# A two-layer scan and mixture-of-experts kernel: expert biases through a selection matmul, C's product on GpSimd, and a second variance worked out from the first

## The reference

```python
x = L0_attn_x
xn = _layernorm(x)                                   # (x - m) / sqrt(v + 1e-5)
x = x + scan_layer(xn) + experts_0(xn)               # layer 0
xn = _layernorm(x)
x = x + heads(xn) + experts_1(xn)                    # layer 1

# scan_layer: 16 states n per channel
h_n[t] = exp(delta[t] * A_n) * h_n[t-1] + delta[t] * x[t] * B_n[t]
y[t]   = sum_n C_n[t] * h_n[t]
return y + D_param * x

# experts_l: 8 experts, the best 2 per token
h   = gelu(x @ w1[n] + b1[n])                        # 128 -> 512
out = h @ w2[n] + b2[n]                              # 512 -> 128
# experts_1 alone normalises its input once more:
xn2 = (x - mu) / sqrt(var + 1e-5) * gamma + beta
```

## Time and profile before

| | us |
|---|---|
| median of 3 runs | 1023.39 (1023.01 to 1023.41) |
| the profiled execution, its time | 1015.58 |
| its span in the trace | 1013.8 |
| busy: PE, DVE | 699.5 (69%), 777.8 (77%) |
| busy: ACT, POOL | 526.4 (52%), 445.8 (44%) |
| mean granted TensorE clock | 0.809 of full speed |

### The profile page before, as it was taken

The page is one execution under the profiler, slowest core; times in us unless marked ns, Lnnn a source line. Parts: engine busy times, 40 slices in busy tenths (PEclk is TensorE's granted clock), DMA queues, the critical chain, the costliest instruction groups (busy, mean ns, idle before and its releaser), DMA issues.

```text
span 1013.8 us, 18728 instructions
## 1 busy us (share of the span) xinstructions
PE 699.5 (69%) x5012; PEld 470.6 (46%) x5012; DVE 777.8 (77%) x1700; ACT 526.4 (52%) x1131; POOL 445.8 (44%) x444
## 2 busy tenths in 40 slices
PE   1975176789998999889901451259789789788760
PEld 0422022256565555556601351237667567567550
DVE  4898999989889888989657729535786775876857
ACT  2678423387768776875304520054664564655620
POOL 1356385634454444444202551525555555554330
PEclk9865578899999999999965555568798797797775
DMA  8332132434444444343150020001111011111108
GB/s 243 110 95 68 40 92 76 128 107 127 117 130 112 121 117 122 112 124 109 61 158 21 1 83 1 11 21 30 31 31 33 29 29 30 31 35 28 23 10 248
DMA packets 68658, 78.56 MB, mean 77 GB/s; under 512 B 10354, under 2 KB 43576, under 8 KB 68564
## 3 DMA queue, kind: packets, MB, share of 16 engines
q1 hardware_dynamic: 55124, 57.42, 19.7%
q0 software_dynamic: 9216, 17.85, 7.0%
q10 hardware_dynamic: 4224, 2.10, 0.7%
HBM read 62.39 MB, written 15.99 MB: 77 GB/s over the span
## 4 chain that ended last, share of the span: by engine, by line
PE 40%; DVE 34%; issue 12%; ACT 6%; POOL 3%; DMA 2%; SPq 1%; another core or an unknown queue 1%; DVEq 0%; ACTq 0%; POOLq 0%
PE pb L767 7%; PE po L812 6%; PE pb L912 6%; DVE work L1196 5%; DVE x L1084 3%; PE ph L793 3%; PE po L810 3%; DVE work L1205 2%; DVE work L1343 2%; PE ph L795 2%; PE ph L794 2%; DVE pb L1188 2%; PE po L817 2%; PE pb L903 2%; PE po L819 1%
## 5 line engine op out<-in xcount | busy, mean ns | idle before, releaser
L465 POOL DMA_INDIRECT results<-res,pair_of x144 | 156.0, 1084 | 305.8 <-DVE res L1159 283.2
L593 ACT ACTIVATE arena<-ph,b 128x128 f32<-128x128 f32 x576 | 164.7, 372 | 142.6 <-PE ph L795 87.4
L459 POOL DMA_INDIRECT xrow<-rows,row_of x144 | 159.5, 1108 | 64.2 <-issue 42.1
L1196 DVE TENSOR_TENSOR_SCAN work<-decay,pb 128x512 f32<-128x512 f32 x128 | 154.7, 1208 | 0.1
L767 PE MATMUL pb<-work,idf 128*128 128x512 f32 x256 | 140.7, 638 | 5.2 <-DVE work L1205 4.4
L793 PE MATMUL ph<-xrT,w1h 128*128 128x128 f16 x576 | 123.7, 233 | 25.4 <-issue 15.0
L794 PE MATMUL ph<-xrT,w1h 128*128 128x128 f16 x576 | 122.3, 231 | 0.0
L795 PE MATMUL ph<-xrT,w1l 128*128 128x128 f16 x576 | 122.2, 230 | 0.0
L570 ACT ACTIVATE decay<-big,avec 128x510 f32<-128x510 f32 x128 | 83.0, 710 | 47.0 <-DVE work L1196 46.7
L578 ACT COPY xrT<-px 128x512 f16<-128x512 f16 x72 | 42.3, 588 | 110.7 <-PE px L778 97.9
L1159 DVE COPY res<-po 128x128 f32<-128x128 f32 x144 | 40.9, 284 | 72.4 <-PE po L819 43.5
(11 more groups left out here) (196 smaller groups left out, 1542.7 us busy)
## 6 DMA issues: line engine op xcount, KB each, us to landing
work<-c_rows SPq DMA_DIRECT2D x64, 256.0 KB
c_ring<-c_rows SPq DMA_DIRECT2D x64, 256.0 KB
decay<-in_w SPq DMA_DIRECT2D x24, 256.0 KB, 3.0
rows<-rows SPq DMA_DIRECT2D x16, 256.0 KB, 2.3
decay<-results SPq DMA_DIRECT2D x16, 256.0 KB, 4.1
big<-results SPq DMA_DIRECT2D x16, 256.0 KB, 4.8
xrow<-rows,row_of POOLq DMA_INDIRECT x144
results<-res,pair_of POOLq DMA_INDIRECT x144
```

Source lines behind the costliest of these rows:

```text
L459: e.indirect_dma_start(xrow[:, b % XR, :], None, rows_dram[l], bass.IndirectOffsetOnAxis(row_of[:, b:b + 1], 0)).then_inc(s_row[b % XR], 16)
L465: e.indirect_dma_start(res_dram[l], bass.IndirectOffsetOnAxis(pair_of[:, b:b + 1], 0), res[:, b % RR, :], None, bounds_check=NRES - 1, oob ...
L593: ins = e.activation(dst[:, c * P:(c + 1) * P], ph[:, b % 2, c * P:(c + 1) * P], ACT.Gelu, bias=b1[:, col(en * HC + (l * NE * HC + c))])
L1196: e.tensor_tensor_scan(work[:, 2 + n % 2, :], decay[:, n, :], pb[:, at % 3, :], 0.0, ALU.mult, ALU.add).then_inc(s_scan, 1)
```

## The change

Four things, made together.

1. **Biases by selection.** b1 of both layers is loaded twice, turned once by TensorE, and kept as 128 rows of 128 (`b1_parts`: rows from 0 the fp16 high parts, rows from 64 the remainders); b2 likewise (`b2_parts`). `chosen` is a 0/1 matrix. One matmul of 512 columns starts `block_up`'s sum with b1, and one of 128 columns starts `block_down`'s with b2, in place of two one-row matmuls. Six more small loads are made, and `b2_in` goes from VectorE.
2. **Gelu.** One activation of 512 columns in place of four of 128; ScalarE no longer reads the block's expert number.
3. **C's product.** From group 1 on `weigh` runs on GpSimd, in place, between its gathers and scatters; group 0 keeps it on VectorE. States lie in PR = 4 slots, `scan` waits for the `y_sum` four steps back, `y_sum` runs three steps behind (SUMLAG), and `skip` and `end_scan` of a group move to steps 2 and 3 of the next. GpSimd waits for the row indices at step 3 of group 1 (FETCHED).
4. **Second factor.** The variance of a normalised row is (v) / (v + eps), so it is worked out from the first one; the statistics of the normalised tensor go, and ScalarE makes the factor after the second group is normalised. gamma enters with the factor in one instruction per tile (`scaled`), beta in one per group (`shifted`).

```diff
-                      (b1[:, 0:NE * HC], a["b1_0"]), (b1[:, NE * HC:2 * NE * HC], a["b1_1"]),
+            small += [(b1[:, (2 * k + l) * NE * HC:(2 * k + l + 1) * NE * HC], a[f"b1_{l}"])
+                      for k in range(2) for l in range(2)]
+            small += [(b2_raw[64 * k + l * NE:64 * k + (l + 1) * NE, :], a[f"b2_{l}"].rearrange("o (n d) -> (o n) d", n=NE))
+                      for k in range(2) for l in range(2)]
...
+                for at in range(NS, GROUPS * NS) if l == 0 else ():
+                    if at == NS + FETCHED:
+                        indices_in(0)
+                        for b in range(AHEAD):
+                            fetch(b)
+                    if (tick := tick_at(at // NS, at % NS)) is not None:
+                        blocks_tick(tick)
+                    weigh(at)
...
-                for c in range(HC):
-                    ins = e.activation(dst[:, c * P:(c + 1) * P], ph[:, b % 2, c * P:(c + 1) * P], ACT.Gelu,
-                                       bias=b1[:, col(en * HC + (l * NE * HC + c))])
-                ins.then_inc(s_gelu, 1)
+                e.activation(dst, ph[:, b % 2, :], ACT.Gelu).then_inc(s_gelu, 1)
...
+            e.wait_ge(s_var, 3)
+            st.seq(e.activation(tmp2, var2, ACT.Ln))
+            e.activation(rstd2, tmp2, ACT.Exp, scale=-0.5).then_inc(s_rstd, 1)
...
+                e.matmul(ph[:, b % 2, :].rearrange("p (c t) -> p c t", c=HC), b1_parts[:, :],
+                         chosen[:, bass.ds(en * HC + l * NE * HC, HC)].unsqueeze(2).to_broadcast([P, HC, P]),
+                         start=True, stop=False)
...
-                for k in range(2):
-                    e.matmul(o, ones_h[:, :], b2_parts[:, bass.ds(en * (2 * D) + k * D, D)], start=(k == 0), stop=False)
+                e.matmul(o, chosen[:, bass.ds(en + l * NE, 1)].to_broadcast([P, P]), b2_parts[:, :],
+                         start=True, stop=False)
...
+                    if n < SUMLAG and g > 0:
+                        y_sum(g - 1, NS - SUMLAG + n)
+                    if n == SUMLAG and g > 0:
+                        to_tokens(g - 1)
+                    if n == SUMLAG + 1:
+                        y_sum(g, 0)
+                    if n > SUMLAG:
+                        y_sum(g, n - SUMLAG)
...
-                if n >= 2:
-                    e.wait_ge(s_prod, at - 1)
+                if at >= PR:
+                    e.wait_ge(s_ysum, at - PR + 1)
...
-            for g in range(0, GROUPS):
+            st.seq(e.tensor_tensor(tmp2, rstd[:, :], rstd[:, :], ALU.mult))
+            st.seq(e.scalar_tensor_tensor(out=tmp2, in0=vare[:, :], scalar=-LN_EPS, in1=tmp2,
+                                          op0=ALU.add, op1=ALU.mult))
+            e.tensor_scalar(var2, tmp2, LN_EPS, None, ALU.add).then_inc(s_var, 1)
...
+            def scaled(g):
+
                 e.wait_ge(s_xn, g + (GROUPS + 1))
-                st.done(stats_of(work_all, g))
-            st.wait()
-            moments(3)
...
+                    ins = e.scalar_tensor_tensor(out=big[:, at], in0=work_all[:, at], scalar=rstd2[:, i:i + 1],
+                                                 in1=gb[:, 0, :], op0=ALU.mult, op1=ALU.mult)
+                ins.then_inc(s_xf, 1)
...
+            def shifted(g):
+
                 e.wait_ge(s_xf, g + 1)
...
+                e.tensor_tensor(v, v, gb[:, 1, :].unsqueeze(1).to_broadcast([P, TG, D]), ALU.add).then_inc(s_gb, 1)
```

More of the change, by code:

```diff
@@ L467, in send, with blocks_tick @@
                                          oob_is_err=False).then_inc(s_sent[b % RR], 16)
-                for b in range(AHEAD):
-                    fetch(b)
-                for tick in range(BLOCKS + DRAIN):
+                def blocks_tick(tick):
                     if tick + AHEAD < BLOCKS:
@@ L475, in _, with weigh @@
                         send(b)
+                def weigh(at):
+                    e.wait_ge(s_c[at % CR], 16 * (at // CR + 1))
+                    e.wait_ge(s_scan, at + 1 + NS)
+                    e.tensor_tensor(product_row(at), product_row(at), c_row(at), ALU.mult).then_inc(s_prod, 1)
+                for at in range(NS, GROUPS * NS) if l == 0 else ():
[6 more added lines that the diff above has]
+                    weigh(at)
+                if l == 1:
+                    indices_in(1)
+                    for b in range(AHEAD):
+                        fetch(b)
+                for tick in range(BLOCKS + DRAIN) if l else range(BLOCKS, BLOCKS + DRAIN):
+                    blocks_tick(tick)
         @block.scalar
@@ L623, in scan_group @@
                     for tick in range(BLOCKS, BLOCKS + DRAIN):
-                        blocks_tick(0, tick, expert)
+                        blocks_tick(0, tick)
             e.wait_ge(s_wlo, 2 * NE)
@@ L766, in y_sum @@
                     e.wait_ge(s_att, g + 1)
-                e.matmul(py, idf[:, :], work[:, 4 + n % 2, :], start=(n == 0), stop=(n == NS - 1))\
+                e.matmul(py, idf[:, :], product_row(g * NS + n), start=(n == 0), stop=(n == NS - 1))\
                     .then_inc(s_ysum, 1)
@@ L1211, in begin_scan, with skip_in @@
                 drive(g, 0)
+            def skip_in(g):
+                e.wait_ge(s_ysum, (g + 1) * NS)
+                e.scalar_tensor_tensor(out=yT, in0=xT[:, group(g)], scalar=cols[:, 1:2], in1=py,
+                                       op0=ALU.mult, op1=ALU.add).then_inc(s_yT, 1)
             def end_scan(g):
@@ L1229, in scan_group @@
                         rows_at(0)
[L1230 to L1231 removed]
+                    if n >= 1 and g == 0:
                         weigh(g, n - 1)
[L1233 removed]
+                    if n == SUMLAG - 1 and g > 0:
+                        skip_in(g - 1)
+                    if n == SUMLAG and g > 0:
                         end_scan(g - 1)
[L1235 removed]
+                if g == 0:
+                    weigh(g, NS - 1)
                 if g + 1 < GROUPS:
                     begin_scan(g + 1)
[L1238 to L1240 removed]
                 if g == GROUPS - 1:
+                    skip_in(g)
                     for tick in range(BLOCKS, BLOCKS + DRAIN):
@@ L1287, in _ @@
+            def shifted(g):
+                e.wait_ge(s_xf, g + 1)
+                v = big[:, group(g)].rearrange("p (t c) -> p t c", t=TG)
+                e.tensor_tensor(v, v, gb[:, 1, :].unsqueeze(1).to_broadcast([P, TG, D]), ALU.add).then_inc(s_gb, 1)
+            for g in range(GROUPS):
+                scaled(g)
+                if g > 0:
+                    shifted(g - 1)
+            shifted(GROUPS - 1)
             e.wait_ge(s_lg, 2 * GROUPS)
```

132 lines of the change are left out of this document (58 added, 74 removed).

## The result

The changed kernel takes 987.34 us (median of 4 runs, 985.53 to 989.63) where the kernel before takes 1023.25 beside it: ratio 0.965, interval 0.963 to 0.9671, 36 us faster. The profiled execution took 987.72 us with a span of 986.0. Against the old trace (1013.8) that is 27.8 us. The other 8 us are the distance of the old profiled execution (1015.58) from its own median, which the changed kernel doesn't have (987.72 against 987.34).

The account below looks back on a forecast made before the run. Three bounds: TensorE's pace in the scan (GpSimd's after the change), VectorE's run in the middle, VectorE and TensorE alternately in layer 1. Terms 2.5 - 5.8 + 7.2 + 1.5 - 0.5 - 9.6 + 3.0 = -1.7 gave 1021.7 us, range 1001 to 1045.

Parts of the forecast that it names:

- Opener: Start of the kernel: six more small loads, all on the chain, cost +2.5 us, bounds +1.8 and +2.9.
- Group 1: Scan's group 1: row indices about 2.3 us earlier, GpSimd ends at 210.3 instead of 216.1, -5.8 us.
- Groups 2 to 6: Scan: GpSimd becomes slowest with products between gathers and scatters, 244 us in all, +7.2; bounds from -6.7 up.
- group 7: Scan's last group: last product follows the last recurrence on another engine, and `y_sum` follows it, +1.5 us.
- Middle: Normalisation to router: VectorE's and GpSimd's work added up, remainder rows end at 579.5 not 589.1, -9.6 us.
- Layer 1: Layer 1's eight groups: ticks cost 1.0 us a group, shorter gelu returns 0.5; +3 us, bounds -5 and +8.
- The gelu's half microsecond a group: Layer 1: shorter gelu gives back 0.5 us a group, where TensorE's part ends in a block VectorE waits for.
- From the trace to the median: Whole kernel: sums made against the profiled execution; the runs' median lies 7.81 us above it, added at the end.
- B: Rival, scan: GpSimd does not set the pace, groups 2 to 6 fall to 230.2 us, total 1007.9; chance 0.20.
- C: Rival, scan: pause before a gather is 0.81 us, sum +29.3, total 1052.7 us; chance 0.18.
- D: Rival, middle: it saves nothing, remainder rows begin as late as before, sum +7.9, total 1031.3 us; chance 0.12.
- E: Rival, layer 1: added matmuls keep the granted clock up and gain 21 us; chance 0.08.

Follow-up runs that it names:

- a2_after_third: The changed kernel itself, unaltered, run a third time, at the lower level: 981.81 us, ratio 0.986 to the kernel before.
- h3a: Changed kernel with only group 1's products on GpSimd, all others on VectorE, lag of three and in-place products kept: 955.31 us, again 952.36, lower level.
- e1b: Changed kernel with part 4 undone (second statistics taken from the rows again), second time, upper level: 1002.95 us beside the changed kernel's 986.95.
- e11: Changed kernel with part 2 of its edits undone alone: b2 fetched and split before each layer, two one-row matmuls per block; 994.82 us, lower level.
- e10: Changed kernel with the first bias undone alone: b1 as a column of four gelus again, no matmul for it; 981.04 us, lower level.
- e4: Changed kernel with four gelus of 128 columns for one of 512, without bias or expert number on ScalarE: 987.76 us, upper level.
- a0_after_here: The changed kernel itself, unaltered, on the chip of the experiments, at the upper level: 988.09 us, ratio 0.968 to the kernel before.
- e2_products_on_vector: Changed kernel with part 3 undone (all scan products on VectorE, two-step lag, rings of two), lower level: 965.44 us, ratio 0.966 to the kernel before.
- e2b_products_on_vector: Changed kernel with part 3 undone (all scan products on VectorE, two-step lag), second time, upper level: 986.94 us beside the changed kernel's 986.95.
- h1: Changed kernel with products shared: GpSimd keeps group 1, 9 steps of group 2, later only the five steps without a gather; 994.94 us, upper level.

## Why the prediction was wrong

The steps that failed most are the adding-up of VectorE's and GpSimd's work in the middle (6.8 us), the sizes of the two changed matmuls in layer 1 (10.9 us), the pauses in GpSimd's queue in the scan (7.2 us) and the 7.81 us that were added for the median. For each term the forecast's value stands first.

- **Opener**, +2.5: the traces have +4.3 at the start of group 1. "All of this is on the chain" was mis-sized: the first step of VectorE behind the loads starts 0.65 us later (20.01 for 19.36), not 2.5. Another 2.6 us come up before the scan starts (122.83 for 119.56 in all), and 1.0 in group 0 (50.6 us for 49.6), of which the forecast had nothing. What they are stays open. The granted clock from 46 us to 94 is 0.50 for 0.61, but it doesn't settle it: with 0.62 there the same program starts the scan at 122.1 (a2_after_third), and h3a, one program twice, starts it at 120.2 and 123.1 with 0.62 and 0.61.
- **Group 1**, -5.8: -7.8 at VectorE's border. That the two are near is partly luck. The estimate took GpSimd's own end, 210.3, or 212.8 with the opener; GpSimd ended at 217.04. The step that failed is that the row indices "come about 2.3 us earlier": they were made 10.5 us after the group's start for 10.7 before (183.98 - 173.44 and 179.79 - 169.14). From there GpSimd needed 32.0 us, forecast 32.8. VectorE's border lies 4.5 us ahead of GpSimd's end, and that gave the -7.8.
- **Groups 2 to 6**, +7.2: -3.8, and group 7, +1.5: +5.3. The sum of the two is +1.5 for +8.7. That GpSimd sets the pace was right, with it over VectorE's and TensorE's. No row of before had shown at what pace products go beside VectorE's work: the 64 of groups 3 to 6 took 1.30 us each, for 1.27 taken. The size failed in "I stay with 0.30", and in the 0.5 us for uneven steps. The pauses are 0.16 before a gather and none behind a scatter, the steps are even, and so a group has 47.8 us for 49.3. On GpSimd itself groups 2 to 6 last 453.59 - 217.04 = 236.6 us, which is 54 x 3.79 + 26 x 1.23, for 244 forecast and 236.9 before. Group 2 is only 41.8 us long at VectorE's border because VectorE's lead grows there from 4.5 to 7.9 us, and group 7 is longer because its skip waits for the last product.
- **Middle**, -9.6, bounds -15 and 0: -16.4 in the traces, 16.0 by e1b. The step that failed is "so I add them up". VectorE's run took 23.1 us (552.71 to 575.8) for the sum's 20.8, and that it ended near the sum's 577.0 is luck, since the whole stretch lies 3.5 us earlier. But the remainder rows didn't wait for that end: they ran from 566.28 between VectorE's instructions, not up to 579.5 behind them. Nor was GpSimd shut out as at 574.09 of the earlier trace rows. Its additions took 1.26 to 1.74 us each, for 1.27 before. VectorE's four-instruction pieces took 2.0 to 3.2 us where GpSimd was at work beside them, and 1.13 for the last, alone. VectorE's run has no gap in either trace, yet in the old one GpSimd's two instructions took 15.04 us and in the new one the first two remainder rows took 2.49. What makes the one engine's work longer beside the other's, and why it fell out so differently, no run here tells.
- **Layer 1**, +3, bounds -5 and +8: -7.9 with the stretch before it, outside the bounds. Three steps failed. "Loses one of two b2 matmuls (..., half of it latency, so 0.06)" was an estimate of the author's, and mis-sized: it is 0.16 us (0.28 for 0.12 to the next piece of work), and e11 puts it at 9.9 us for seven groups. "Some 4.5 ticks gain 0.16 us each at full clock" took the added matmul, 0.22, as if it counted in full, and it was nearly hidden (1.6 us by e10). The doubling to 0.32 at half clock fits the trace of before: the twelve 128-column matmuls of a block's down-projection follow one another at 0.056 us where the granted clock is 1.00 (from 851.44) and at 0.107 where it is 0.50 (from 844.11). `b2_in` "beside the first gathers: 0" was 1.5 us by e11. The gelu's half microsecond a group was nothing by e4.
- **From the trace to the median.** "Which I add at the end" carried the 7.81 us of the old trace over to the changed kernel, which has none of it. That is 8.2 of the 34.4 us between forecast and result; without it the result still lies below the range.
- **The whole.** With the measured sizes the terms are +4.3 - 7.8 + 1.5 - 1.5 (from the skip to the normalisation) - 16.4 - 7.9 = -27.8 us, which is the traces' difference. The middle and layer 1 make 17.7 of the 26.1 us between it and the forecast's -1.7.
- **The rivals.** B's 230.2 us didn't come, nor C's pause of 0.81 us, which had kept the range high: it is 0.16. D is ruled out by the 16.0 us of e1b. E had the added matmuls keep the granted clock up in layer 1 and gain 21 us, an estimate from the two places of the earlier trace rows, where the granted clock is 0.74 in the mean (0.50 for the first 2 us) and 1.00. Of it there is little: over seven groups of layer 1 the granted clock is 0.88 for 0.85 before, and a0_after_here, with 0.86, takes the same 268.6 us as the first trace of the changed kernel with 0.88 (268.8).
- The scan looks harmless at the upper level only. At the lower the same change is only 1.4% faster, and part 3 is its worst part.

## What to carry to other kernels

Two small additions with the same busy time can have very different prices. Here two matmuls of some 13 us of TensorE's time each cost 1.6 and 9.9 us over the same 63 blocks. Look which wait gets shorter for each, and undo them one by one. When work is moved to an idle engine, add up that engine's queue for the densest stage first: here 11 x 3.79 + 5 x 1.23 us made GpSimd the bound, and leaving the move only in the stage where it had room gave 29 us more at the lower level. A part that costs nothing at one level of the kernel before may be the one to drop.

## What the runs showed of the hardware that was not expected

The same program had two levels. For the kernel before, 16.1 of the 24.6 us between them lie up to the skip of group 7, where TensorE and VectorE are fullest (groups of 44.7 and 47.9 us, granted clock 1.00 in both). But 5.6 lie between the router and layer 1, and in the changed kernel, whose scan is bound by GpSimd, 4.2 of 8.3 us lie there (68.9 for 64.6) and 4.3 in layer 1. In that stretch TensorE is busy for 21.7 of 68.8 us, so a full TensorE is not the condition.

In the scan the added time lies at fixed places. From recurrence to recurrence, groups 3 to 5 of the kernel before grow in the same four steps each: in group 3 from 2.51 to 3.51, 2.91 to 3.51, 2.82 to 4.48 and 2.04 to 3.01 us. In e2_products_on_vector and its second run, another program, the same four steps grow by nearly as much (2.51 to 3.48, 2.82 to 3.48, 2.74 to 4.46, 1.93 to 2.96). Two later steps get some 0.5 to 1.0 us shorter in each.

At the upper level the list of waits has rows whose releaser the trace doesn't show: 44.2 us in the first trace of before, 56.0 in e2b_products_on_vector, 17.0 in the first trace of the changed kernel, where none of them is in the scan. All ten traces of the upper level have such rows, and none of the ten of the lower has one. Two of them in the first trace of before:

```profile
DVE res L1159 <- remote: 20.9, 8, 3.6
ACT arena L593 <- remote: 18.5, 7, 3.7
```

In h1 one such place shows TensorE itself standing. Its timeline, and the stretches around it:

```profile
337.30 0.22 PE L846 MATMUL ph<-xrT,w1l 128*128 128x128 f16 x1
338.00 0.22 PE L844 MATMUL ph<-xrT,w1h 128*128 128x128 f16 x1 [0.49 <-issue]
338.72 0.22 PE L845 MATMUL ph<-xrT,w1h 128*128 128x128 f16 x1 [0.49 <-issue]
339.44 0.22 PE L846 MATMUL ph<-xrT,w1l 128*128 128x128 f16 x1 [0.51 <-issue]
```

```profile
336.00:340.00 4.00, 2.17 (x15) 0.90 (x13) 0.37 (x2) 0.47 (x1) 1.99 (x2) 1.00 0.43 115
340.00:343.50 3.50, 3.34 (x12) 2.66 (x13) 3.50 (x5) 3.47 (x6) 0.00 (x0) 0.52 0.11 43
```

Matmuls that follow at 0.06 us come 0.72 apart without a wait that the trace shows, and right behind them the granted clock is 0.52 of full speed for some 3.5 us. Such a stretch of slow clock comes once in each of groups 3 to 6 of h1. The standing adds 2.1 us in three of them and 0.7 in the fourth, so it is a part of what lies between 50.0 and h3a's 42.9 us, and not all. It isn't the level's cause either: e2b_products_on_vector has one stretch of slow clock in these groups, and the first trace of before has none. What holds TensorE up there, and what makes the levels, stays open: no run was made for it.
